# Second attention of a gated transformer block: row sums of the last four heads move from ScalarE's accumulator to one VectorE reduce

## The reference, cut to what matters

```python
scores = jnp.einsum('bhqd,bhkd->bhqk', Qh, Kh) / scale        # 16 heads of 8 features, 128 x 128 scores each
scores = scores - jnp.max(scores, axis=-1, keepdims=True)
scores = jnp.clip(scores, -CLAMP, CLAMP)
attn = jax.nn.softmax(scores, axis=-1)
attn = jnp.clip(attn, EPS, None)
attn = attn / jnp.sum(attn, axis=-1, keepdims=True)
ctx = jnp.einsum('bhqk,bhkd->bhqd', attn, Vh)
```

## Time and profile before

| | us |
|---|---|
| median of three runs | 3238.92 (3237.65 to 3240.37) |
| the profiled execution, its own time | 3230.85 |
| its span, first to last instruction | 3229.0 |
| granted TensorE clock, mean | 0.989 of full speed |

### The profile page before, as it was taken

The page is one execution under the profiler, slowest core; times in us unless marked ns, Lnnn a source line. Parts: engine busy times, 40 slices in busy tenths (PEclk is TensorE's granted clock), DMA queues, the critical chain, the costliest instruction groups (busy, mean ns, idle before and its releaser), DMA issues.

```text
span 3229.0 us, 137162 instructions
## 1 busy us (share of the span) xinstructions
PE 3114.9 (96%) x59429; PEld 1932.1 (60%) x59460; DVE 2863.7 (89%) x3141; ACT 2448.5 (76%) x4480; POOL 2637.7 (82%) x1430
## 2 busy tenths in 40 slices
PE   7988999999999999999999999999999999998997
PEld 4554666666666666666666666666666666664554
DVE  6888999999999999899999999999999999956888
ACT  6875677777777777777777777777777777767896
POOL 1229999999999999899999989999989999953677
PEclk9998999999999999999999999999999999999998
DMA  3002434444444344443444444444444443440000
GB/s 100 2 2 73 129 119 129 118 120 126 130 126 128 110 126 124 121 129 116 117 124 126 130 127 117 125 118 128 126 120 120 121 124 115 119 152 1 2 12 18
DMA packets 237004, 336.45 MB, mean 104 GB/s; under 512 B 39926, under 2 KB 161140, under 8 KB 236020
## 3 DMA queue, kind: packets, MB, share of 16 engines
q1 hardware_dynamic: 236404, 327.69, 34.5%
HBM read 124.14 MB, written 102.76 MB: 70 GB/s over the span
## 4 chain that ended last, share of the span: by engine, by line
PE 85%; issue 4%; POOL 4%; ACT 3%; DVE 3%; DMA 0%; SPq 0%; POOLq 0%; DVEq 0%; ACTq 0%
PE psum L848 29%; PE psum L919 10%; PE psum L905 9%; PE psum L878 8%; PE psum L946 8%; PE psum L860 6%; PE psum L957 4%; PE psum L936 2%; PE psum L928 2%; POOL f_rotated L1441 1%; POOL f_rotated L1433 1%; ACT x_expo L1853 1%; ACT x_expo L421 1%; PE psum L1678 1%; PE psum L1688 1%
## 5 line engine op out<-in xcount | busy, mean ns | idle before, releaser
L1433 POOL TENSOR_TENSOR f_rotated<-f_times_cos,f_times_sin 128x1024 f32<-128x1024 f32 x384 | 908.8, 2367 | 2.9 <-DVE f_times_sin L1261 2.8
L1441 POOL TENSOR_TENSOR f_rotated<-f_rotated,f_rnorm 128x1024 f32<-128x1024 f32 x384 | 725.5, 1907 | 3.6 <-ACT f_rnorm L1088 3.5
L1097 ACT COPY f_qkT<-psum 128x1024 f32<-128x1024 f32 x384 | 370.6, 1016 | 404.9 <-PE psum L860 404.7
L1260 DVE TENSOR_TENSOR f_times_cos<-psum,f_rot 128x1024 f32<-128x1024 f32 x384 | 469.6, 1223 | 153.1 <-ACT f_squares L1074 151.0
L1425 POOL TENSOR_TENSOR f_probs<-f_probs,f_rowsum 128x1024 f32<-128x1024 f32 x192 | 365.4, 1903 | 242.0 <-DVE f_rowsum L1296 240.3
L1074 ACT ACTIVATE f_squares<-psum 128x1024 f32<-128x1024 f32 x384 | 393.5, 1025 | 186.9 <-PE psum L848 185.8
L848 PE MATMUL psum<-w_qkv,f_xs 128*128 128x512 f32 x1152 | 531.4, 606 | 2.9 <-DVE f_times_sin L1261 1.1
L848 PE MATMUL psum<-w_next,f_xs 128*128 128x512 f32 x1152 | 523.0, 597 | 1.0 <-issue 1.0
L1261 DVE TENSOR_TENSOR f_times_sin<-psum,f_rot 128x1024 f32<-128x1024 f32 x384 | 466.2, 1214 | 0.0
L1268 DVE TENSOR_REDUCE f_sumsq<-f_squares 128x16 f32<-128x1024 f32 x384 | 454.6, 1184 | 0.2 <-issue 0.2
L848 PEld LDWEIGHTS psum<-w_qkv,f_xs 128*128 128x128 f32 x1152 | 217.5, 193 | 263.6 <-issue 256.5
(11 more groups left out here) (184 smaller groups left out, 5650.8 us busy)
## 6 DMA issues: line engine op xcount, KB each, us to landing
f_v_moved<-f_v SPq DMA_DIRECT2D x768, 128.0 KB
turned_blocks<-w_qkv SPq DMA_DIRECT2D x192, 512.0 KB, 2.6
f_probsT<-turned_blocks SPq DMA_DIRECT2D x768, 128.0 KB
w_qkv<-in_l_wqkv SPq DMA_DIRECT2D x36, 128.0 KB, 3.2
w_next<-in_l_wqkv SPq DMA_DIRECT2D x36, 128.0 KB, 2.5
w_o<-in_l_wo SPq DMA_DIRECT2D x6, 512.0 KB, 4.3
w_qkv<-in_ctxT SPq DMA_DIRECT2D x1, 2048.0 KB, 8.8
w<-in_l_w SPq DMA_DIRECT2D x6, 341.0 KB
```

Of the source, the lines that this page charges most:

```text
L1097: act.copy(qkT[u % 2][:, part].rearrange("p t (j n) -> p j t n", j=2), pair(("qT", "kT")[part], u).rearrange("p (j t n) -> p j t n", j=2, ...
L1260: dve.tensor_tensor(by_half(times_cos[part][:, :]), halves(taken), table(0), ALU.mult)
L1433: pool.tensor_tensor(rotated[u % 2][:, part].rearrange("p h d -> p (h d)"), times_cos[part][:, :], times_sin[part][:, :], ALU.add).then_in ...
L1441: pool.tensor_tensor(rt, rt, rnorm[u % 2][:, part * H:(part + 1) * H].unsqueeze(2).broadcast_to([P, H, HD]), ALU.mult).then_inc(normalised ...
```

## The change

The exponentials of heads 12 to 15 of every batch no longer collect their sums. In front of the reciprocals of the second half, VectorE sums these four heads of `expo` in one instruction into `total[:, 12:]` and waits for it on a new semaphore. Heads 0 to 11 are as before.

```diff
+            SUMMED = 12
+            summed, inverted = sem("x1_summed"), sem("x1_inverted")
...
                     for h in range(8 * half, 8 * half + 8):
+                        sums = dict(accum_out=total[b % 2][:, h:h + 1]) if h < SUMMED else {}
                         e = act.activation(expo[b % 2][:, h, :], psum[:, 4 + h // 4, (h % 4) * S:(h % 4 + 1) * S], ACT.Exp,
-                                           bias=negmax[b % 2][:, h:h + 1], accum_out=total[b % 2][:, h:h + 1])
+                                           bias=negmax[b % 2][:, h:h + 1], **sums)
                     e.then_inc(exped[half], 1)
...
                     dve.wait_ge(exped[half], b + 1)
+                    if half == 1:
+                        dve.tensor_reduce(total[b % 2][:, SUMMED:], expo[b % 2][:, SUMMED:, :], axis=X, op=ALU.add).then_inc(summed, 1)
+                        dve.wait_ge(summed, b + 1)
                     dve.reciprocal(t8, t8).then_inc(inverted, 1)
```

More of the change, by code:

```diff
@@ L1543, in second_attention @@
             scored, maxed, exped, normalised = ([sem(f"x1_{k}{half}") for half in range(2)] for k in ("scored", "maxed", "exped", "normalised"))
-            inverted = sem("x1_inverted")
+            SUMMED = 12
+            summed, inverted = sem("x1_summed"), sem("x1_inverted")
             turned, clipped = sem("x1_turned"), sem("x1_clipped")
```

## The result

The changed kernel took 3272.90 us (median of 4 runs, 3265.60 to 3274.61) beside 3238.28 us (3233.07 to 3240.37, 4 runs) of the kernel before: a ratio of 1.0103, with a 95% interval of 1.0082 to 1.0124. The forecast of 3252.4 us, range 3246 to 3259, had the sign and missed the size: some 35 us came where 13.5 were expected. The profiled execution took 3274.37 us, with a span of 3272.6 us at a mean granted clock of 0.978; before it was 3229.0 us at 0.989.

What follows compares the result with a forecast made beforehand. Waits between engines, none of them full, were taken to set the pace; 0.9 + 1.35 + 2.0 + 6.0 + 1.8 + 1.5 = 13.5 us on the 3238.92 us median gave 3252.4 us, range 3246 to 3259.

Steps and rivals of the forecast that it cites:

- What bounds the stage: In the second attention no engine is full; waits between engines set the pace, and VectorE's 4.6 us of waits lie elsewhere.
- A, B and C: First three VectorE reciprocals of head sums in a repeating group (3082.66, 3093.24, 3102.69 us), where other engines wait for VectorE.
- A, +0.67: First reciprocal, between the halves of VectorE's key bias: its reduce delays ScalarE's key biases, transpose and scores by 0.67 us.
- B +1.34 and C +2.01: Delay reaches 1.34 us through quantisation and division behind the second reciprocal, then 2.01 us at TensorE's mix behind the third.
- D costs nothing: Group's fourth reciprocal, at 3109.60 us: a 0.59 us wait for exponentials and a 0.25 us gain cover its reduce.
- The saving per head: ScalarE without accumulator reads on four heads per batch: 0.2 us per batch taken, with 0.37 and nothing as bounds.
- The sum of the groups: Delays of the groups from 2944.49 (+0.9), 2976.40 (+1.35), 3009.22 (+2.0) and the three repeating ones (+6.0 us together).
- The group from 3148.5 and all behind: +1.8 us, the first two reduces overlapping ScalarE waits; from 3183 us on +1.5 us, partly covered.
- The clock: TensorE's granted clock: the sum added nothing for it; a lower clock appeared only in a rival, at most 7 us.
- TensorE's longer waits let its clock fall once more per group: Rival: clock falls behind longer waits, at most 1.4 us each, 7 us over five groups, 3259; shared chance 0.13.
- its sister case: Rival: all 32 reduces land, 21 us, 3260, if the saving brings nothing and fourth reciprocals aren't covered; shared chance 0.13.
- The prediction's own sign of being wrong: Wrong if the granted clock falls below 1.00 in groups behind 3045 us, or a group under 35.2 or over 37.2 us.

Runs made afterwards that it cites:

- e3: The change with the four accumulator reads kept, so only VectorE's reduce and its wait are added: 3261.57 us, ratio 1.0067.
- e2: The change without its reduce: heads 12 to 15 collect no sums, their totals set to one: 3239.55 us, ratio 0.9995.
- e8: The change with TensorE's mean made three times and four transposes three times in each group's last batch: 3256.71 us, ratio 1.0054.
- e4: The change with the second half's reduce, wait and reciprocal moved behind the second key bias: 3252.45 us, ratio 1.0045.
- e1: The kernel before with one more semaphore allocated, which nothing uses: 3236.09 us, ratio 0.9989.
- e5: The change with TensorE's row-mean matmul made twice into the same bank: 3262.24 us, ratio 1.0073.
- e10: The change with two heads (14 and 15) instead of four moved to the reduce: 3260.94 us, ratio 1.0069.
- e11: The kernel before with one more ScalarE key bias, into a spare tile, lengthening TensorE's wait for the key bank: 3255.31 us, ratio 1.0062.
- e6: The change with the second half's reduce and reciprocal moved two clips later: 3246.04 us, ratio 1.0022.
- e7: The kernel before with only the second half's reciprocals moved two clips later, no reduces, reads kept: 3244.52 us, ratio 1.0010.
- e0: The changed kernel run again with no edit: 3264.48 us, ratio 1.0083 to the kernel before.
- e9: The kernel before with TensorE's row-mean matmul made twice: 3241.63 us, ratio 1.0003.

## Why the prediction was right on the path and wrong in size

By its own steps:

- **What bounds the stage** was right. A, B and C are where others wait for VectorE: each delayed what stands behind it by 0.71 to 0.73 us, step by step, and VectorE's 4.6 us of waits hid almost none of it (3.9 us are left in the group shown above).
- **A, +0.67**: +0.73. TensorE's wait in front of the transpose rose from 1.39 to 2.12 us. ScalarE's in front of the key bias rose from 0.74 to 1.85 us, where I expected 1.4: ScalarE arrives sooner, without its reads, and stands longer.
- **B +1.34 and C +2.01**: +1.45 and +2.18. The reduce takes 0.677 us with a gap of 0.03, near the upper bound of 0.72 and not at 0.67.
- **D costs nothing**: right (-0.06 us; its reciprocal came at +2.54 us, where +2.43 was forecast), and e3 shows that the saved reads are a part of its cover.
- **The saving per head** was mis-sized without harm. Four exponentials take 1.00 us from start to start, 0.25 each, against 0.345 with the read: 0.37 us a batch where I took 0.2. The spacing of 294 ns that followed from the Trainium skill ("ScalarE: Activation LUTs", section "What ACT_TABLE_LOAD costs") isn't what this trace shows; the measurement decides. In the repeating groups the saving brings nothing but D's part, as forecast (e2).
- **The sum of the groups**, 0.9 + 1.35 + 2.0 + 6.0 = 10.25 us: with the clock kept (e8) +11.6, a repeating group of 36.59 us against 36.5 forecast.
- **The group from 3148.5 and all behind**, 1.8 + 1.5 = 3.3 us: +4.6 in e8, and 5.2 to 6.1 in the two profiles of the change and that of e4. The path's part was about right: 1.6 of the 4.6 are one short fall more than before, and the other three profiles have more low clock there than before, too. No experiment took the two addends apart.
- **The clock: the step that failed.** The sum leaves the clock as it was, and the rival "TensorE's longer waits let its clock fall once more per group" was priced "at most 1.4 us each, 7 us over five groups" and given 0.13 together with its sister case. The mechanism is the right one, and I had its first instance in the earlier trace rows. The price came from that instance alone: one short fall behind a wait of 1.39 us, and 1.4 us for it was near enough (1.6). What was wrong is "once more per group" and the length. Behind 2.12 us six of the seven falls in the two profiles of the change were long, at 3.1 to 3.2 us each (37.33 and 39.61 us in the change against 34.25 and 36.39 in e8). And there is a second place, the mix behind C with its 1.47 us, which I had named as a longer wait and not as a place for a fall: the group of 39.81 us has two short falls, that of 41.75 a long and a short one. Over the six groups the falls cost 229.69 - 214.09 = 15.6 us in one profile of the change and 12.3 in the other; some of it, 1.3 us in the first group, is the fall at the opening of the stage, which every profile has and which lasted longer here. The prediction's own sign of being wrong, a granted clock below 1.00 in the groups behind 3045 us, came true.

So what was measured comes together as: 16.3 us of e8 over before (some 15 of path, the rest a fall), less the 1.6 us of the fall that the kernel before has already in its third group, plus 12 to 16 us of clock in the groups, plus at most 1.5 us in the rest. That is 28 to 31 us by profile, beside medians 26 and 35 us apart; the stages ahead, untouched by the change, move by up to 20 us between executions and are enough for the difference.

A second reading doesn't hang on single profiles. Each of the 189 executions on record that I compare has its time and its mean granted clock. Among executions of one kernel, 0.001 less of that clock goes with 2.4 us more (one straight slope through all kernels, each with its own level). The line shows what goes together, not what causes what. Read at the same clock of 0.987, which is an estimate good to some 2 us, the kernel before takes 3237 to 3238 us in each of its four sets and e1 3237. The change takes 3253 and 3254, e3 and e5 3255, e8 with its added work 3256, e4 and e10 3247, e11 3245, e6 3242, e7 3240 and e2 3232. So at equal clock the change costs 16 us in both of its measurements, near the 13.5 of the forecast, and what is left of 26 and 35 us goes with a mean clock of 0.982 and 0.980 instead of about 0.986. It also places the 10 us of e11: 7 us at equal clock, and 13 with a clock of 0.983 instead of 0.988. And it shows two heads at 9 us of path, where four cost 16.

Four runs make the cause more than a fit: filling TensorE's waits with useless work makes the changed kernel faster (e8), taking the reduce out of the longer wait gives 12 to 15 us, 5 to 7 of them path (e4), the falls come without any reduce when the wait is lengthened otherwise (e11), and the new semaphore is innocent (e1).

What stays open is why some waits are followed by a fall and others not: the same 2.12 us were harmless at 3114.91 in the change, twice in e0 and three times in e3, and in e10 1.20 us was not. TensorE's work just ahead of a wait differs a little from group to group, and no run varied that alone; it can't be all, since the fourth group of the change fell in one execution and not in the other. The Trainium skill ("TensorE: Matmul & The Clock Gate", section "A second HAM failure mode: psum-queue depth-cycling") says that a kernel which lets TensorE idle briefly and often between groups of matmuls makes its clock go back and forth between the two levels. The traces here agree: 1.2 to 2.1 us of standing in a stage where TensorE is busy 87% of the time. No version was faster than the kernel before beyond its interval; e6 came nearest of those with the reduce, at 1.0022.

## What to carry to other kernels

Where an engine looks as if it had room, find where its waits lie: an instruction put in front of what another engine waits for costs its full length, once for each such place, and the idle time elsewhere doesn't pay for it. When a change makes TensorE stand longer, price the clock apart from the delay, by more than one instance and at every place where it stands: here it cost nearly as much again as the delay. And if such a wait can't be removed, redundant matmuls that end before the awaited data arrive are a cheap trial; here they gave some 10 us.

## What the runs showed of the hardware

- The granted clock fell to 0.50 behind waits of TensorE of 1.2 to 2.1 us, in a stage where TensorE works nearly all the time: behind 7 of 10 waits of 2.12 us, 3 of 8 of 1.47 us (two profiles of the change), and 1 of 5 of 1.39 us (before). Over the six groups of all fourteen profiles 33 falls begin, and each does so between 0.2 us ahead of and 2.2 us behind the end of a TensorE wait of 1.2 us or more: 13 of 20 waits of 2.05 to 2.12 us, 2 of 5 of 1.85, 9 of 23 of 1.40 to 1.48, 5 of 30 of 1.31 to 1.39, none of 5 of 1.26 (e5), 4 of 5 of 1.20 (e10). In e8 and e9, whose waits there are at most 0.91 and 1.06 us, none begins.
- A short fall of about 3 us cost 1.5 to 1.6 us of the group, a long one of about 7 us 3.1 to 3.2 (e1, e11, and the change against e8).
- An accumulator read adds 0.09 us to the start-to-start time of a 128x128 exponential from PSUM (0.343 against 0.25 us), half of its own recorded duration of 0.19 us.
- A reduce over 128x512 fp32 takes 0.677 us as a sum, where a maximum of the same shape takes 0.634, with GpSimd at work beside both.
